# Two products a chunk, and halves added ahead of the relu, for the half empty up tile of the last unit

## The reference, cut to what matters

```
w_up = dequant_nf4(w_up_codes, w_up_absmax, (H, D)).T        # D = 1024, H = 2752
y1 = x1 @ w_up + b_up + x1 @ w_up_lora_a @ w_up_lora_b
x2 = jax.nn.relu(y1)
w_down = dequant_nf4(w_down_codes, w_down_absmax, (D, H)).T
y2 = x2 @ w_down + b_down + x2 @ w_down_lora_a @ w_down_lora_b
```

## Time and profile before

| | |
|---|---|
| runs | 1436.6, 1438.92 and 1445.63 us; median 1438.92 us |
| profiled execution, span | 1438.6 us (no separate time of it is given) |
| PE busy | 1398.8 us, 97% of the span, 6817 matmuls |
| DVE busy | 1137.8 us, 79% |
| ACT busy | 755.7 us, 53% |
| mean granted clock of PE | 0.994 of full speed |

### The profile page before, as it was taken

One profiled execution on the slowest core, in us unless ns is written; L12 is line 12 of the kernel. 1 busy time (PEld: TensorE's weight loads), 2 busy tenths in 40 slices (PEclk: granted clock), 3 DMA queues, 4 the chain that ended last, 5 costly groups with the idle time before them and its releaser, 6 DMA issues.

```text
span 1438.6 us, 20752 instructions
## 1 busy us (share of the span) xinstructions
PE 1398.8 (97%) x6817; PEld 1146.1 (80%) x6817; DVE 1137.8 (79%) x1101; ACT 755.7 (53%) x839; POOL 211.0 (15%) x218
## 2 busy tenths in 40 slices
PE   7899999999999999999999999999999899999996
PEld 7888888888888888888888888887755688888785
DVE  6869887878877787887878878787644699999895
ACT  5655554545546455464554644643123277777672
POOL 0111000000000000000000000000011266665443
PEclk9999999999999999999999999999999999999998
DMA  6864656568665686656865667756668547969951
GB/s 221 315 223 165 236 209 254 196 250 273 237 246 203 234 292 229 227 218 227 294 240 206 240 220 281 256 191 240 238 231 287 160 121 194 354 190 303 332 146 35
DMA packets 102680, 331.48 MB, mean 230 GB/s; under 512 B 15220, under 2 KB 22908, under 8 KB 102620
## 3 DMA queue, kind: packets, MB, share of 16 engines
q1 hardware_dynamic: 79556, 258.56, 48.4%
q0 software_dynamic: 22816, 71.85, 17.9%
q10 hardware_dynamic: 256, 0.40, 0.1%
HBM read 295.63 MB, written 46.14 MB: 238 GB/s over the span
## 4 chain that ended last, share of the span: by engine, by line
PE 85%; DMA 6%; DVE 3%; issue 2%; ACT 2%; SPq 0%; ACTq 0%; POOL 0%; DVEq 0%; POOLq 0%
PE pair L1133 26%; PE pair L1135 26%; PE pair L1134 25%; PE pair L1187 4%; DMA z_rows<-z 3%; DMA wraw<-exp_w 3%; PE pair L1402 1%; DVE wf L808 1%; PE pair L1214 1%; PE pair L1271 1%; PE pair L1197 1%; ACT z L718 1%; DVE wlr L1108 1%; PE pair L1369 1%; PE pair L1183 1%
## 5 line engine op out<-in xcount | busy, mean ns | idle before, releaser
L808 DVE TENSOR_TENSOR wf<-wf,term 128x1024 f32<-128x1024 f32 x308 | 376.7, 1223 | 65.7 <-ACT term L593 50.5
L593 ACT ACTIVATE term<-codes 128x1024 f32<-128x1024 int32 x308 | 320.6, 1054 | 139.4 <-DVE wf L808 139.4
L1133 PE MATMUL pair<-wh,hh 128*128 128x512 f32 x672 | 263.4, 392 | 3.2 <-DVE ring L871 1.4
L1134 PE MATMUL pair<-wl,hh 128*128 128x512 f32 x672 | 262.0, 390 | 0.0
L1135 PE MATMUL pair<-wh,hl 128*128 128x512 f32 x672 | 262.0, 390 | 0.0
L1133 PE MATMUL pair<-ring,wh 128*128 128x512 f32 x656 | 255.5, 390 | 0.0
L1134 PE MATMUL pair<-ring,wh 128*128 128x512 f32 x656 | 255.3, 389 | 0.0
L1135 PE MATMUL pair<-ring,wl 128*128 128x512 f32 x656 | 255.2, 389 | 0.0
L741 ACT ACTIVATE whr<-wraw 128x1024 fp32r x184 | 187.9, 1055 | 85.3 <-PE pair L1135 50.8
L866 DVE TENSOR_TENSOR acc<-acc,pair 128x1024 f32<-128x1024 f32 x160 | 194.4, 1216 | 47.2 <-PE pair L1135 39.8
L1108 DVE TENSOR_TENSOR wlr<-wraw,whr 128x1024 fp32r<-128x1024 f32 x184 | 213.3, 1215 | 12.5 <-ACT whr L741 12.2
(11 more groups left out here) (178 smaller groups left out, 1527.6 us busy)
## 6 DMA issues: line engine op xcount, KB each, us to landing
ring<-x_parts SPq DMA_DIRECT2D x320, 512.0 KB, 6.4
wraw<-exp_w SPq DMA_DIRECT2D x64, 512.0 KB, 11.2
x_parts<-stage POOLq DMA_DIRECT2D x24, 512.0 KB, 6.0
xg<-exp_b POOLq DMA_DIRECT2D x23, 512.0 KB, 8.0
codes<-codes_up SPq DMA_DIRECT2D x22, 512.0 KB, 5.8
codes<-codes_dn SPq DMA_DIRECT2D x22, 512.0 KB, 5.6
am<-am_dn SPq DMA_DIRECT2D x22, 512.0 KB, 3.7
acc<-x_nat POOLq DMA_DIRECT2D x16, 512.0 KB, 5.5
```

The lines of the kernel that those rows point to most:

```text
L593: return nc.scalar.activation(out, codes[:, n % 2], ACT.Relu, scale=scale, bias=-scale * bend)
L808: nc.vector.tensor_tensor(whole(n), whole(n), term[:, e % 2], op).then_inc(term_added, 1)
L1133: mm(ps, ah, bh, start=first, stop=False)
L1134: mm(ps, ah, bl, start=False, stop=False)
```

## The change

In chunks 1, 2 and 3 of the last unit the half empty up tile is computed in another way. Its `wh` columns 64 to 127, which held a copy of columns 0 to 63, are overwritten with the low parts (`both_parts`, DVE). Then two products a kt, this joint tile with the high part and with the low part of x1, go into bank[1] in place of three. Partitions 0 to 63 then hold the high weights' sum and partitions 64 to 127 the low weights' sum. ACT copies each half to the other half's partitions of `swapped`, DVE adds `swapped` to bank[1], and the relu of bank[1] follows. Chunk 0 stays as it was.

```diff
+            def last_relu(q):
+                i = UNITS // 2
+                act.wait_ge(up_mm, i * 8 + q + 1)
+                nc.scalar.activation(bank[0], bank[0], ACT.Relu, bias=bup[:, NT - 2:NT - 1]).then_inc(relu_done, 1)
+                for h in range(2):
+                    wait(act, halves_added, q - 1)
+                    nc.scalar.activation(swapped[h * 64:(h + 1) * 64], bank[1][(1 - h) * 64:(2 - h) * 64],
+                                         ACT.Copy).then_inc(swapped_ready, 1)
+                act.wait_ge(halves_added, q)
+                nc.scalar.activation(bank[1], bank[1], ACT.Relu, bias=bup[:, NT - 1:NT]).then_inc(relu_done, 1)
                 wait(act, dn_mm, i * 32 + 4 * (q - 1))
                 act.wait_ge(relu_done, i * 16 + 2 * (q + 1))
                 h = 2 * (q % 2)
...
             high(UNITS // 2, 3)
-            relu(UNITS // 2, 1)
+            last_relu(1)
             perceptron(0)
             perceptron(1)
-            relu(UNITS // 2, 2)
+            last_relu(2)
             perceptron(2)
-            relu(UNITS // 2, 3)
+            last_relu(3)
...
             low(UNITS // 2, 3)
+
+            def both_parts():
+
+                dve.wait_ge(up_mm, 4 * (UNITS - 1) + 1)
+                dve.wait_ge(wl_ready, 4 * (UNITS - 1) + 2)
+                nc.vector.tensor_copy(high_part(1).rearrange("p (k n) -> p k n", n=P)[:, :, 64:P],
+                                      low_part(1).rearrange("p (k n) -> p k n", n=P)[:, :, 64:P]).then_inc(both_parts_ready, 1)
+
+            def add_halves(q):
+                dve.wait_ge(swapped_ready, 2 * q)
+                nc.vector.tensor_tensor(bank[1], bank[1], swapped[:], ALU.add).then_inc(halves_added, 1)
+
+            both_parts()
             dve.wait_ge(bdn_in, 16)
...
                 if k < NC - 1:
+                    add_halves(k + 1)
                     hidden_low(UNITS // 2, k + 1)
...
+            def last_up(q):
+
+                i = UNITS // 2
+                pe.wait_ge(both_parts_ready, 1)
+                pe.wait_ge(hl_ready, i * 8 + q)
+                for kt in range(KT):
+                    pe.wait_ge(x1_in[kt], i * 128 + 16 * (q - NC + 1))
+                    c = slice(kt * P, (kt + 1) * P)
+                    three(bank[0], high_part(0)[:, c], low_part(0)[:, c], ring[:, kt, 0], ring[:, kt, 1],
+                          kt == 0, kt == KT - 1)
+                    for part in range(2):
+                        ins = mm(bank[1], high_part(1)[:, c], ring[:, kt, part], start=kt == part == 0,
+                                 stop=kt == KT - 1 and part == 1)
+                    if kt < KT - 1:
+                        ins.then_inc(x1_used, 1)
+                return ins
...
                 if k < NC - 1:
-                    up(UNITS // 2, k + 1).then_inc(up_mm, 1)
+                    last_up(k + 1).then_inc(up_mm, 1)
                     perceptron(2 * k)
```

More of the change, by code:

```diff
@@ L151, in program @@
         aggs = sb(tail, "aggs", [P, 2 * 512])
+        swapped = sb(tail, "swapped", [P, CHUNK])
         tail.close()
@@ L268, in program @@
         up_mm, relu_done, hh_ready, hl_ready = sem("up_mm"), sem("relu_done"), sem("hh_ready"), sem("hl_ready")
+        both_parts_ready, swapped_ready, halves_added = sem("both_parts_ready"), sem("swapped_ready"), sem("halves_added")
         dn_mm, acc_added = sem("dn_mm"), sem("acc_added")
@@ L633, in relu @@
                 nc.scalar.activation(hh[:, h:h + 2], pair[0][:].rearrange("p (s t) -> p s t", s=2), ACT.Copy).then_inc(hh_ready, 1)
+            def last_relu(q):
[8 more added lines that the diff above has]
+                nc.scalar.activation(bank[1], bank[1], ACT.Relu, bias=bup[:, NT - 1:NT]).then_inc(relu_done, 1)
+                wait(act, dn_mm, i * 32 + 4 * (q - 1))
+                act.wait_ge(relu_done, i * 16 + 2 * (q + 1))
+                h = 2 * (q % 2)
+                nc.scalar.activation(hh[:, h:h + 2], pair[0][:].rearrange("p (s t) -> p s t", s=2), ACT.Copy).then_inc(hh_ready, 1)
             def conv_high(k):
```

## The result

In the first measurement the changed kernel took 1445.53 us in the median of 20 runs, the kernel before 1441.86 us (20 runs); the ratio is 1.0028, 95% interval 1.0015 to 1.0041, that is 4.0 us more (2.2 to 5.9). The forecast was 1445.1 us and 6.2 us more. So the kernel does less work on the bound engine and is slower.

The account below looks back on a forecast made before the run. The last unit was taken as bound by PE in `up` and by an ACT and DVE chain in `last_down`. Saved matmuls -5.4, wait +3.2, chain +5.0, clock +3.4 gave +6.2 us, so 1445.1 us, range 1439.0 to 1450.0.

Parts of the forecast that it names:

- The bound: Last unit: PE bounds `up`, a chain over ACT and DVE the middle of `last_down`; 24 matmuls saved, 5.44 us.
- The wait ahead of `up` 1: PE waits for `both_parts`, queued on DVE behind `add_down` and `low`: 3.2 us lost, 2.7 with the lower end.
- The chain: Behind each `up`, ACT and DVE steps grow by 1.9 us (1.3 to 2.2); together 5.0 us lost.
- `last_down` 2: Chunk 2, row tile j = 2: 0.7 us of slack go first, 1.2 us of longer chain are left.
- PE asks for it at 1048.49: In `last_down` 2, PE needs the first `add_down` at 1048.49 us; it ends at 1047.74, giving 0.7 us of slack.
- The clock: Behind PE's waits of 3.0 and 2.8 us the granted clock falls: 2 x 1.7 = 3.4 us, 0 to 5.1.
- The base: Whole kernel before: profiled span 1438.6 us, median of the runs 1438.92, 0.3 above it.
- (a): Rival: the clock holds at 2.4 GHz through all waits, +2.8 us, 1441.7 us; chance 0.20.
- (b): Rival: the experts' stage takes up the delay, 4.2 us come back, 1437.5 us, not slower; chance 0.13.
- a stage of the experts that changes by more than 2 us: Sign against the forecast: the experts' stage's own length changes by more than 2 us.
- (c): Rival: only PE's saved work counts, the two waits are hidden, 1433.5 us; chance 0.02.
- (d): Rival: the clock doesn't recover between waits from `up` 1 on, 62 us more, 1504 us; chance 0.02.

Follow-up runs that it names:

- e4: Kernel before with only the two products a chunk, low part of the half empty tile's weights left out: last unit 70.09 us, ratio 0.9970.
- e2: Kernel before plus only a DVE copy to a tile nobody reads, which PE awaits ahead of `up` 1: last unit 80.03 us, ratio 1.0049.
- e8: Changed kernel with both_parts on ACT, down bias loaded first and the joint tile's 16 products first in `up`: last unit 68.63 us, ratio 0.9925.
- e10: The same kernel as e8 measured again, against the kernel before: last unit 68.63 us, ratio 0.9967.
- e9: The changed kernel measured again, against the kernel before: last unit 81.15 us, ratio 1.0059.
- e1: Changed kernel with both_parts done by ACT in its idle time ahead of `high`: last unit 80.44 us, ratio 1.0036 to the kernel before.
- e5: Changed kernel with 12 unused matmuls ahead of PE's wait for both_parts: last unit 81.10 us, one run only.
- e6: e1 with the down bias loaded ahead of the nine small loads of the mix: last unit 76.55 us, ratio 1.0015 to the kernel before.
- e3: Kernel before with only the longer chain, a DVE maximum in place of the add, three products: last unit 80.41 us, ratio 1.0040.
- e7: e6 with ACT's two copies ahead of the relu of bank 0: last unit 74.43 us, one run only.

## Why the prediction was right

The forecast held in its sign, its time and nearly all its steps. In its own terms, -5.4 + 3.2 + 5.0 + 3.4 = +6.2 us, the last unit had -5.4 + 2.9 + 5.0 + 3.2 = +5.7.

- **The bound.** The saved matmuls were all on the path: 5.4 us by e4, as predicted.
- **The wait ahead of `up` 1.** 3.2 us were predicted, 2.94 measured. The queue on DVE was as read; the term that was mis-sized is the copy, 0.42 us and not 0.69. Here the estimate from the Trainium skill, VectorE: DVE Perf Modes, section on the perf-mode tier table, was the better guide: it made the copy about 0.3 us shorter, and the trace agrees with 0.27 (0.69 less 0.42). The row of a two-input operation with as many elements was the wrong neighbour.
- **The chain.** 1.9 us were predicted, 2.09 measured (3.42 - 1.33). A copy of half the partitions took 0.59 us, as one of all. Two steps from start to start were taken too short: the first copy began 0.69 us behind the first relu, not 0.58, and the second 0.62 us behind the first (1.21 for both, less one of 0.59), not 0.52, so neither overlapped the operation ahead of it. PE's waits grew by 1.7 us in `last_down` 0 and 2.0 in 1. They grew by less than the chain because ACT also started its first relu sooner: 0.03 us behind the end of the last matmul, as the timelines count it, against 0.43 before in job 1, and 0.04 against 0.12 in job 2. The old `relu` has a semaphore increment between its wait and its first operation which the new one lacks. It has it in both jobs, though, so it can't be the whole of the 0.43; the cause stays open.
- **`last_down` 2.** 1.2 us predicted, 0.97 + 0.19 measured, but by another mechanism. The step that failed is "PE asks for it at 1048.49": I looked at the `add_down` alone. `aggregate` stands ahead of j = 2 and waits for `aggb`, which DVE makes behind the same split, so the chain reached PE there first. Before, `aggb` was done by 1046.49 us and `aggregate` began at 1047.50 without a wait, 1.0 us of slack; after, `aggb` came at 1054.31 and PE waited. The timelines of DVE and PE before, and of DVE after:

```profile
1046.13 0.36 DVE L777 COPY aggb<-pair 64x16 f32<-64x16 f32 x2
```

```profile
1047.50 1.06 PE L1170 MATMUL pair<-kerns,att_t 8*32 8x512 f32 x8
```

```profile
1054.31 0.36 DVE L794 COPY aggb<-pair 64x16 f32<-64x16 f32 x2
```

- **The clock.** Two falls were predicted, of 1.7 us each, and two came, of 1.6 (by e2) and 1.5. The rule that I read from two rows, long waits fall and short ones don't, is too simple, though (below), so that the count was right is partly luck.
- **The base.** I added 0.3 us to the span for what lies around it. The runs after give time and span side by side: 1441.32 and 1439.8 us, so it is 1.5. And the median of three runs of before, 1438.92, was 3 us below that of 20. The predicted time of 1445.1 hit 1445.53 because a base 2.9 us too low met a difference forecast 2.5 us above the 3.7 between the medians. That the time came out within 0.5 us is luck; the 0.5 us by which the last unit's 5.7 misses the 6.2 is what the mechanism can claim.

Of the rivals, (a) a clock that holds is out by the windows of the changed kernel. (b), the experts' stage takes up the delay: in the profiled execution what follows the last unit was 6.3 us shorter, but both measurements show the changed kernel slower. By the prediction's own signs, a stage of the experts that changes by more than 2 us would have shown it wrong. That sign was set too tight, since the same kernel profiled twice differs there by 8.6 us (e8 and e10). (c) and (d) are out: both waits are real, and the clock recovered each time.

## What to carry to other kernels

A saved instruction on the bound engine has to be weighed against what it asks of the others at the same place: here 5.4 us of matmuls cost 5.0 us of longer chain, 2.9 us of a wait behind an in-order queue, and 3.2 us for two falls of the clock. A dependent step of another engine is cheap if the work that feeds it is done first and the rest of the bound engine's work covers it; the same products in another order, with the copy of the low parts given to idle ACT and the bias loaded earlier, turned +5.7 us into -6.8 (e8). Where runs scatter by more than the edit is worth, the length of the stage that the edit touches, read from the timelines, tells what the median can't.

## What the runs showed of the hardware that I had not expected

- **The same wait doesn't always bring the clock down.** By the granted clock of the windows behind them, in the last unit of the 14 profiles: waits of PE of 2.79 us were followed by a fall three times of three (changed, e2, e9), one of 3.34 us too (e1); waits of 2.87 to 2.89 us four times of six (changed, e5, e6, e9, but not e1 and e3); waits of 2.12 to 2.19 us two times of six (e5 and e7, but not the changed kernel, e3, e6 and e9); and in e1 the clock even fell 0.6 us behind a wait of 0.98 us and one of 0.19, which five other runs passed without one. A fall cost 1.5 to 1.7 us, but 2.7 us behind the 3.34 us in e1, where the clock stayed down for longer. The Trainium skill, TensorE: Matmul & The Clock Gate, section on why this matters for your kernels, puts the limit at idle gaps of about 3 us; here it is no safe limit, since waits of 2.1 us fell twice.
- **Filling one wait moved the fall.** With the wait at `up` 1 filled (e5, a single execution), the clock held there and fell at a wait of 2.12 us, of a length that it had passed in the changed kernel (2.13).
- **A copy on ACT costs the same for 64 partitions as for 128:** 0.59 us for 64x512 (the six copies of the changed kernel) against 0.60 for 128x512.
